# A graph layer's scatter-add on one core: gathers spread otherwise over the program, and TensorE told to take the high halves first

## The reference

```
h    = x @ W_in2f
Wij  = (ssp(edge_attr_64 @ Wf1 + bf1) @ Wf2 + bf2) * edge_weight1
x_ij = h[dst] * Wij
m    = segment_sum(x_ij, src, num_segments=N)
m    = ssp(m @ Wo1 + bo1) @ Wo2 + bo2
out  = layernorm(x + x + m)            # over the 256 features
```

## Time and profile before

| | us |
|---|---|
| median of 3 runs (lowest, highest) | 1823.19 (1818.78, 1825.59) |
| the profiled execution, its own time | 1837.85 |
| its span, first to last instruction | 1836.1 |
| first transposes of step 14, 75, 97 | 214.15, 1045.71, 1338.59 |
| first scatter starts | 207.15 |
| second loop's first transposes | 1382.97 |

### The profile page before, as it was taken

One profiled execution on the slowest core, in us unless ns is written; L12 is line 12 of the kernel. 1 busy time (PEld: TensorE's weight loads), 2 busy tenths in 40 slices (PEclk: granted clock), 3 DMA queues, 4 the chain that ended last, 5 costly groups with the idle time before them and its releaser, 6 DMA issues.

```text
span 1836.1 us, 36487 instructions
## 1 busy us (share of the span) xinstructions
PE 1740.3 (95%) x11376; PEld 1543.6 (84%) x11376; DVE 1507.6 (82%) x3750; ACT 1484.6 (81%) x2945; POOL 1429.4 (78%) x1385
## 2 busy tenths in 40 slices
PE   4989999999999999999999999999978999999995
PEld 3778888888888888888888888888877999999995
DVE  3777877888878888778888788888866999999996
ACT  3777877778787787777787888888757999999996
POOL 5554688888888888888888877777764999999997
PEclk9999999999999999999999999999988999999998
DMA  9999866666666666666666656777655899999994
GB/s 340 373 385 392 218 120 119 114 120 121 115 121 118 119 121 115 122 121 115 121 118 116 119 109 113 155 148 154 127 88 193 288 361 362 360 362 361 362 362 171
DMA packets 177340, 363.45 MB, mean 198 GB/s; under 512 B 25623, under 2 KB 76265, under 8 KB 177149
## 3 DMA queue, kind: packets, MB, share of 16 engines
q1 hardware_dynamic: 101128, 257.75, 40.7%
q0 software_dynamic: 75136, 102.45, 34.0%
q10 hardware_dynamic: 884, 0.92, 0.2%
HBM read 206.90 MB, written 154.12 MB: 197 GB/s over the span
## 4 chain that ended last, share of the span: by engine, by line
PE 23%; POOL 23%; issue 3%; DMA 2%; ACT 1%; DVE 1%; another core or an unknown queue 0%; POOLq 0%; ACTq 0%; DVEq 0%
PE pair L411 15%; POOL sums L387 14%; POOL to_spare L383 5%; PE pair L497 4%; POOL acc L356 2%; PE pair L422 2%; POOL to_spare L381 1%; PE pair L435 1%; PE pair L434 1%; DMA acc<-sums,src_ix 1%; DMA xg<-in_x,dst_t 1%; DVE msg_l L674 0%; ACT zs L584 0%; ACT zs L578 0%; POOL xg L343 0%
## 5 line engine op out<-in xcount | busy, mean ns | idle before, releaser
L356 POOL DMA_INDIRECT acc<-sums,src_ix x392 | 631.9, 1612 | 163.6 <-issue 103.2
L343 POOL DMA_INDIRECT xg<-in_x,dst_t x392 | 394.8, 1007 | 184.8 <-issue 110.3
L387 POOL TENSOR_SCALAR sums<-sums,to_spare 128x256 f32<-128x256 f32 x392 | 283.1, 734 | 10.2
L623 ACT ACTIVATE m_h<-pair,wgt_t 128x256 fp32r<-128x256 f32 x392 | 164.5, 476 | 133.8 <-PE pair L411 98.6
L497 PE MATMUL pair<-m_h,same 128*128 128x256 f32 (+1 forms) x980 | 252.2, 291 | 7.1 <-issue 3.6
L497 PE MATMUL pair<-m_l,same 128*128 128x256 f32 (+1 forms) x980 | 244.8, 284 | 0.0
L411 PE MATMUL pair<-wo_h,msg_h 128*128 128x256 f32 (+1 forms) x784 | 233.5, 298 | 10.7 <-DVE m_l L784 7.3
L497 PEld LDWEIGHTS pair<-m_h,same 128*128 128x128 f32 (+1 forms) x980 | 187.3, 191 | 41.9 <-DVE m_l L784 20.7
L411 PE MATMUL pair<-wo_h,msg_l 128*128 128x256 f32 (+1 forms) x784 | 222.3, 284 | 0.0
L411 PE MATMUL pair<-wo_l,msg_h 128*128 128x256 f32 (+1 forms) x784 | 221.4, 282 | 0.0
L767 DVE SCALAR_TENSOR_TENSOR pair<-pair,bias_w,h_sb 128x512 f32<-128x512 f32 x196 | 147.9, 755 | 89.2 <-PE pair L411 62.2
(11 more groups left out here) (104 smaller groups left out, 5563.2 us busy)
## 6 DMA issues: line engine op xcount, KB each, us to landing
acc<-fill SPq DMA_DIRECT2D x197, 256.0 KB
xg<-in_x SPq DMA_DIRECT2D x97, 512.0 KB
sums<-acc SPq DMA_DIRECT2D x97, 512.0 KB, 6.9
out<-sums SPq DMA_DIRECT2D x97, 512.0 KB, 4.8
attr<-in_edge_attr SPq DMA_DIRECT2D x196, 128.0 KB
srcb<-in_src_rows SPq DMA_DIRECT2D x98, 256.0 KB
xg<-in_x,dst_t POOLq DMA_INDIRECT x392
acc<-sums,src_ix POOLq DMA_INDIRECT x392
```

The source lines that it names most:

```text
L343: pool.indirect_dma_start(xg[0:g.p, g.xs, r], None, t["x"], bass.IndirectOffsetOnAxis(ap=dst_t[0:g.p, r, g.n:g.n + 1], axis=0)).then_inc(x ...
L356: pool.indirect_dma_start(acc, bass.IndirectOffsetOnAxis(ap=src_ix[g.slot][0:g.p, r:r + 1], axis=0), sums[0:g.p, g.slot, r], None, compute ...
L387: last = pool.tensor_scalar(normed[0:g.p, g.n % NRING, r], res[0:g.p, u, r], neg_mean[0:g.p, u, r:r + 1], rstd[0:g.p, u, r:r + 1], ALU.add ...
L623: act.activation(m_h[0:g.p, r], bank[6][0:g.p, k * D:(k + 1) * D], ACT.Copy, scale=col(wgt_t, r, g)).then_inc(mh_sb, 1)
```

## The change

Three edits, all in the first loop.

1. AHEAD is 28. In the head the wait for a landing stands at the first gather of a group, not at the third, and is for the group two back, not for the one before.
2. After the scatters of group n the gathers go to AHEAD*R + 7*min(n+1, 66)//2 plus a slower part: 3.5 gathers a group for the first 66 groups, then 1.75 a group for the next 28. All are issued after group 93, as before.
3. In `out1`, TensorE takes the 8 matmuls with `msg_h` first and then the 4 with `msg_l`, and `out1(0)` waits for `msg_l` only between the two. In `summed`, all matmuls with `m_h` come first, and the wait for `m_l` stands between. The number and the shapes of the matmuls stay.

```
@@ -48,7 +48,8 @@
-AHEAD = 27
+AHEAD = 28
+TURN = 66
@@ -337,8 +338,8 @@
                     if r == 0:
                         wait(pool, xt_ps, (g.n - XRING + 1) * 2)
-                    if r == 2 and 0 < g.n < AHEAD:
-                        b = group(g.n - 1)
+                    if r == 0 and 1 < g.n < AHEAD:
+                        b = group(g.n - 2)
                         pool.wait_ge(xg_in[b.xs], xg_count(b))
@@ -370,7 +371,9 @@
-                gather_to(AHEAD * R + (n + 1) * (G - AHEAD) * R // (G - 4))
+                fast = AHEAD * R + min(n + 1, TURN) * 7 // 2
+                slow = (G * R - AHEAD * R - TURN * 7 // 2) * max(n + 1 - TURN, 0) // (G - 4 - TURN)
+                gather_to(fast + slow)
@@ -471,31 +474,35 @@ out1(q)
                     if q == 0:
-                        pe.wait_ge(msgl_sb, g.n * H + H)
+                        pe.wait_ge(msgh_sb, g.n * H + H)
                     wait(pe, ml_sb, g.n * R + 2 * q)
                     for k in range(2):
-                        last = three(bank[6][0:g.p, k * D:(k + 1) * D], ...
+                        for h in range(H):
+                            for w in (wo1_h, wo1_l):
+                                pe.matmul(bank[6][0:g.p, k * D:(k + 1) * D], msg_h[:, h, 2 * q + k, 0:g.p], w[:, h],
+                                          start=k == 0 and h == 0 and w is wo1_h, stop=False)
+                    if q == 0:
+                        pe.wait_ge(msgl_sb, g.n * H + H)
+                    for k in range(2):
+                        for h in range(H):
+                            last = pe.matmul(bank[6][0:g.p, k * D:(k + 1) * D], msg_l[:, h, 2 * q + k, 0:g.p], wo1_h[:, h], ...
@@ summed(q)
-                    pe.wait_ge(ml_sb, g.n * R + 2 * q + 2)
+                    pe.wait_ge(mh_sb, g.n * R + 2 * q + 2)
                     ...
-                    for k in range(2):
-                        b = 2 * q + k
-                        for a in range(b + 1):
-                            for m in (m_h, m_l):
+                    for m in (m_h, m_l):
+                        if m is m_l:
+                            pe.wait_ge(ml_sb, g.n * R + 2 * q + 2)
+                        for b in (2 * q, 2 * q + 1):
+                            for a in range(b + 1):
```

More of the change, by code:

```diff
@@ L473, in stage @@
                     if q == 0:
-                        pe.wait_ge(msgl_sb, g.n * H + H)
+                        pe.wait_ge(msgh_sb, g.n * H + H)
                     wait(pe, ml_sb, g.n * R + 2 * q)
                     for k in range(2):
-                        last = three(bank[6][0:g.p, k * D:(k + 1) * D],
-                                     [msg_h[:, h, 2 * q + k, 0:g.p] for h in range(H)], [msg_l[:, h, 2 * q + k, 0:g.p] for h in range(H)],
-                                     [wo1_h[:, h] for h in range(H)], [wo1_l[:, h] for h in range(H)])
+                        for h in range(H):
[6 more added lines that the diff above has]
+                        for h in range(H):
+                            last = pe.matmul(bank[6][0:g.p, k * D:(k + 1) * D], msg_l[:, h, 2 * q + k, 0:g.p], wo1_h[:, h], start=False, stop=k == 1 and h == H - 1)
                     last.then_inc(m_ps, 1)
@@ L489, in stage @@
                     wait(pe, y_sb, g.n * 2 + q)
-                    for k in range(2):
-                        b = 2 * q + k
-                        o = bank[7][0:g.p, k * D:(k + 1) * D]
-                        for a in range(b + 1):
-                            for m in (m_h, m_l):
-                                last = pe.matmul(o, same[0:g.p, FROM[a] + b - a, 0:g.p], m[0:g.p, a],
-                                                 start=a == 0 and m is m_h, stop=a == b and m is m_l)
+                    for m in (m_h, m_l):
[3 more added lines that the diff above has]
+                            for a in range(b + 1):
+                                last = pe.matmul(bank[7][0:g.p, (b - 2 * q) * D:(b - 2 * q + 1) * D], same[0:g.p, FROM[a] + b - a, 0:g.p], m[0:g.p, a],
+                                                 start=b == 2 * q and a == 0 and m is m_h, stop=a == 2 * q + 1 and m is m_l)
                     last.then_inc(y_ps, 1)
```

## The result

| | kernel before | changed kernel |
|---|---|---|
| median of the timed runs, first chip | 1818.95 us (5 runs, 1817.64 to 1825.59) | 1832.11 us (5 runs, 1830.15 to 1834.12) |
| profiled execution, its span | 1837.85, 1836.1 us | 1830.64, 1828.9 us |
| TensorE's step 14 begins | 214.15 us | 213.09 us |
| first scatter | 207.15 us | 199.99 us |
| step 92 begins | 1269.96 us | 1220.17 us |

The ratio is 1.0058 [1.0041, 1.0076]: slower by 0.6% (the medians above stand 0.7% apart), where I had forecast 0.7% faster. Of all the timed runs behind this text one, of 4255.79 us in `x_late`, stands far apart from its kernel's others and is left out.

What follows compares the result with a forecast made beforehand. Bound by a ring of engines through out1(0)'s wait for msg_l, by POOL's drifting bursts before group 74, and by DMA in the head. 4.8 - 19.0 - 1.5 + 5 - 2.3 = -13.0 us: median 1823.19 to 1810 us, range 1800 to 1830.

Steps and rivals of the forecast that it cites:

- Part 1: TensorE's out1 and summed: out1(0) no longer held by msg_l, 0.25 us off each of 76 steps, 19.0 us less.
- Gathers stay ahead of the transposes by over three groups throughout: First loop: gathers keep a lead of over three groups on TensorE's transposes, and no ring wait bites.
- part 3: Rate of gathers in the first loop: longer drifting costs 5 us more, earlier last gathers save 2.3 us.
- GpSimd's 10.0 us a group after group 66: First loop: GpSimd's time a group falls from 12.27 us in the first 66 groups to 10.0 after.
- TensorE's 13.38 us while drifting: First loop: TensorE's step while GpSimd's bursts drift through it, 13.63 - 0.25 = 13.38 us.
- 2.3 us less: End of the first loop: last gathers complete sooner, so TensorE waits less in steps 95 to 97; bounds 0 and 2.7.
- drift's term (+5): First loop: GpSimd locks to the step at group 84 instead of 73; eleven more drifting steps at 0.44 us, 5 us more.
- rival D: First loop: drifting costs nothing of its own, so the 5 us fall away, 1805 us; chance 0.05.
- rival C: First loop: drifting costs more, at twice 0.44 us a step over 73 steps 32 us more, 1842 us; chance 0.10.
- head's term (+4.8): Head: faster gathers delay the clears and src loads on full DMA engines; step 14 4.8 us later, bounds 0 and 9.
- The first scatter at 204: End of the head: clears, no longer gathers, set the first scatter, at 204 us instead of 207.15.

Runs made afterwards that it cites:

- x_late: old_head_even with the second loop's 16 loads of x issued in the second loop instead of the first; 1822.34 us, 0.9934 of the kernel before.
- order_only: The kernel before with only the change's TensorE order (high halves first in out1 and summed); 1819.56 us, 0.9944.
- old_head_even: The changed kernel with the old pacing of gathers in the head and one rate of 2.98 gathers a group; 1824.88 us, 0.9938.
- old_head: The changed kernel with the old pacing of gathers in the head alone; 1852.89 us, 1.0102 of the kernel before.
- spread: old_head_even with one of a group's gathers issued between its second and third scatter; 1899.36 us, 1.0354 of the kernel before.

## Why the prediction was wrong, by its steps

**Part 1 was right in its mechanism, and too large in its sum.** I forecast 0.25 us off each undisturbed step; it is 0.28 (13.19 to 12.91), in `out1` alone, with `out1(0)` at 0.79 us behind the turn. But I counted it for 76 steps, 19.0 us, and the order alone gives 0.6%, some 10 us: the drifting steps keep only half of it (13.31 against 13.44 us in the mean).

**The step that failed on the first chip is "Gathers stay ahead of the transposes by over three groups throughout".** It stood on two terms of part 3. GpSimd's 10.0 us a group after group 66 was 12.0, because the second loop's loads hold the scatters' landings (13.2 us a group with a load in each step, 10.2 to 10.5 before and behind); I had costed the rate from GpSimd's own instructions and not looked at what else the queues carry from step 82 on. And TensorE's 13.38 us while drifting was 12.91. Together they used up the lead at step 92, and the five steps behind it lost 46 us. "2.3 us less" for the last gathers was 42 us more: steps 92 to 96 took 110.6 us, 68.6 in the profile of before. The 50 us that the 78 steps had given, against the first profile of before, went back.

**The drift's term (+5) failed both ways.** On the first chip drifting cost nothing (78 steps of 12.91), as rival D had it; on the others steps 14 to 75 took 13.94 and 13.82 us, 1.0 and 0.9 above the undisturbed 12.91 where I had put 0.44. That is the size at which I had priced rival C, twice 0.44. Its reasons don't hold. The shorter step alone doesn't bring it: 13.31 us in `order_only`, 13.34 in `old_head_even`. Nor do denser bursts behind group 66, where the steps are at 12.9. It goes with 3.5 gathers a group instead of 3 (13.96 in `old_head`), and C named that nowhere. I gave C 0.10 and D 0.05. The rule of the Trainium skill, "SBUF — State Buffer", SBUF: two separate sides, that I weighed under D, agrees with the first chip, where ScalarE has no late start; on the others ScalarE's late starts (30.6 and 29.1 us of "remote" in the changed kernel) speak against taking ScalarE as untouched by GpSimd's work, by whatever way that comes. What I took for a property of the kernel's phases, from a single profiled execution, differs between measurements of one program, and the chip is the likely reason, not a shown one. The chips with the late starts are also those on which the kernel before takes 1830 to 1837 us rather than 1819; but `spread` has none of them on such a chip. That the first profile of before (1837.85 us, 21.5 us of "remote") came from such a chip and its timed runs from another is likely, but only argued.

**The head's term (+4.8) failed.** On the first chip the loads of `src` were later, as I wrote: step 5 came 6.6 us later. All of it came back by step 14 (-1.1). On the other chips step 14 began 45 to 47 us later than before (261.41 and 261.57 us against 215.84 and 214.15), which no row of before showed. The first scatter at 204 was 200.0 on the first chip and 236 to 239 on the others.

**The sum by ratios**, away from the first chip: order -0.6%, pacing in the head +2.2 to +2.6%, rate +1.6 to +1.8%, 28th group not to be told from 0; together +3.2 to +3.8% where 3.0 and 3.4% were measured. By its parts the change is one gain and two losses.

On what bounds: theory P had GpSimd's chain set the end, theory T TensorE's waits. In all 18 profiles the second loop's first transposes come 43.6 to 46.3 us behind those of step 97, whatever GpSimd's pace. So the end follows TensorE's last step, and GpSimd's chain lengthens the kernel where TensorE waits for its gathers: above all in the changed kernel on the first chip and in `spread`.

Open: what holds the handoffs back; why one chip did not show it; and how much of the first chip's 13 us is the starvation alone, since no later run was like it, and the kernel before has no profile there that agrees with its timed runs.

## What to carry to other kernels

A rate for one engine's background work must be checked against the faster step that the same change brings, and against everything that enters the queues later in the loop: the lead at the end is a difference of two large numbers. Loosening the pace of one engine's DMA issues is not free even when the DMA engines are full anyway; try each part alone before the sum. And before costing a mechanism from one profiled execution, look whether that execution's time agrees with the median.

## What I had not expected of the hardware

While GpSimd issues a gather each 1.25 us (16 in 20 us), other engines' starts come 6 to 27 us after what they wait for; at 12 to 13 in 20 us they don't, and on the first chip they did not at 15 to 16. A 0.9 us break in each four gathers makes the single delays shorter and more; step 14 then comes some 40 us late instead of 50. In the loop, rows of three or four gathers ahead of a scatter go with delays of 1 to 5 us, more with four. Four scatters of 128 rows need at least 10.2 us a group here, landing included, of which two gathers fill the rest and each further one costs 1.2 to 1.3. One load of 512 KB in a step holds these landings back by up to 4 us, 2.7 in the mean (13.2 against 10.5 us a group). Sixteen such loads, 8.4 MB, cost nothing in the second loop. The same kernel before took 1818.95 to 1836.85 us, 1% apart, on the chips measured, and 1829.87 and 1834.98 on one of them at two times.
